# Layer 1's experts on their chosen rows only: routing and scattering inside the first plain cross attention, then 39 blocks of 512 rows from a table made on the chip

## The reference, cut to what matters

```python
x = x + L1_xattn(layernorm(x), ctx, ...)        # 16 heads, 77 keys a sequence
x = x + L1_ffn(layernorm(x), ...)

def L1_ffn(xt):                                  # 8192 tokens; D = H = 128, E = 8, K = 2
    scores = softmax(xt @ gate_w.T)              # over 8 experts
    top_vals, idx = top_k(scores, 2)
    xs = xt[:, None, :] * top_vals[:, :, None]
    for e in range(8):
        mask = (idx == e)
        h  = silu(xs @ w1[e].T + b1[e])
        x2 = h @ w2[e].T + b2[e]
        x3 = xs @ w3[e].T + b3[e]
        y += sum over k of x2 * x3 * mask
    z = (silu(xt @ sw1.T) * (xt @ sw2.T)) @ sw3.T   # shared expert, 256 wide
    return y + z
```

## Time and profile before

| what | value |
|---|---|
| time, median of 3 runs | 4141.17 us (4141.11 to 4141.33) |
| the profiled execution's own time | 4179.66 us |
| its span in the trace | 4177.9 us |
| PE busy over the span | 3262.2 us, 78% |
| DVE busy | 3183.3 us, 76% |
| ACT, POOL busy | 2340.8 us (56%), 1688.6 us (40%) |

### The profile page before, as it was taken

One profiled execution on the slowest core, in us unless ns is written; L12 is line 12 of the kernel. 1 busy time (PEld: TensorE's weight loads), 2 busy tenths in 40 slices (PEclk: granted clock), 3 DMA queues, 4 the chain that ended last, 5 costly groups with the idle time before them and its releaser, 6 DMA issues. The chain is left out here.

```text
span 4177.9 us, 77148 instructions
## 1 busy us (share of the span) xinstructions
PE 3262.2 (78%) x23624; PEld 1971.2 (47%) x23624; DVE 3183.3 (76%) x12412; ACT 2340.8 (56%) x4408; POOL 1688.6 (40%) x1692
## 2 busy tenths in 40 slices
PE   4777776999899969999979996886777777676168
PEld 1222222444477744444456664554555555554056
DVE  6999996666588865556578875886999999997055
ACT  5999995333366634444446654664666666665020
POOL 5777773000100012222244444223246666666650
PEclk9999998999899989999999998998555555655575
DMA  2000004100000000000000000000001100000037
GB/s 71 5 5 5 5 5 174 70 1 1 7 9 8 9 25 1 1 1 1 1 17 15 15 13 4 2 2 11 12 27 46 39 18 6 5 4 2 9 95 203
DMA packets 112625, 98.97 MB, mean 24 GB/s; under 512 B 65004, under 2 KB 95928, under 8 KB 109277
## 3 DMA queue, kind: packets, MB, share of 16 engines
q1 hardware_dynamic: 88670, 78.97, 6.7%
q0 software_dynamic: 14336, 10.87, 0.8%
q10 hardware_dynamic: 9216, 4.20, 0.4%
HBM read 55.57 MB, written 57.97 MB: 27 GB/s over the span
## 5 line engine op out<-in xcount | busy, mean ns | idle before, releaser
L393 PE MATMUL PS<-IDENT,a_T 128*77 128x128 f32 (+1 forms) x3584 | 618.0, 311 | 149.1 <-ACT a_Pr L528 115.4
L1012 ACT ACTIVATE l_H<-l_H 128x2048 f32<-128x2048 f32 (+2 forms) x256 | 597.9, 2719 | 2.8 <-POOL l_H L1064 2.7
L393 PEld LDWEIGHTS PS<-IDENT,a_T 128*77 128x77 f32 (+1 forms) x3584 | 480.4, 170 | 249.1 <-issue 91.7
L1064 POOL TENSOR_TENSOR l_H<-l_feat,l_text 128x4096 f32<-128x4096 f32 x64 | 450.6, 7041 | 131.0 <-PE PS L968 130.3
L968 PE MATMUL PS<-l_H,l_wide 128*32 128x512 f32 (+1 forms) x2560 | 331.9, 594 | 165.4 <-ACT l_H L1012 165.3
L1086 DVE TENSOR_TENSOR l_H<-PS,l_text 128x2048 f32<-128x2048 f32 (+1 forms) x192 | 411.6, 2146 | 2.1 <-ACT l_text L1039 2.1
L530 ACT ACTIVATE a_Pr<-PS 77x512 f32<-77x512 f32 (+1 forms) x640 | 375.3, 587 | 53.9 <-PE PS L393 53.7
L408 PE MATMUL PS<-a_Pr,a_vaug 77*32 77x128 f32 (+1 forms) x7168 | 307.2, 317 | 7.6 <-issue 3.1
L2099 POOL DMA_INDIRECT expert_rows<-e3r_row,e3r_rows_at x256 | 254.3, 993 | 86.6 <-issue 73.5
L616 POOL TENSOR_TENSOR a_T<-a_mx,a_T 128x616 f32<-128x616 f32 x128 | 155.7, 1217 | 313.9 <-DVE a_mx L682 313.8
L338 PE MATMUL PS<-a_kblk,a_qT 32*128 32x308 f32 (+1 forms) x2048 | 238.6, 540 | 23.9 <-ACT a_kblk L542 6.6
(11 more groups left out here) (302 smaller groups left out, 8307.1 us busy)
## 6 DMA issues: line engine op xcount, KB each, us to landing
expert_shares<-e_zero SPq DMA_DIRECT2D x16, 1024.0 KB, 22.6
e3c_four<-expert_shares SPq DMA_DIRECT2D x64, 256.0 KB, 3.3
e_w<-in_L_ffn_w SPq DMA_DIRECT2D x14, 512.0 KB
e3x_xin<-expert_rows SPq DMA_DIRECT2D x32, 200.0 KB
expert_rows<-e_zero SPq DMA_DIRECT2D x6, 1024.0 KB, 8.7
a_cT<-in_ctxT SPq DMA_DIRECT2D x128, 38.5 KB, 1.8
X<-in_x SPq DMA_DIRECT2D x8, 512.0 KB, 7.2
expert_rows<-e3r_row,e3r_rows_at POOLq DMA_INDIRECT x256
```

The lines of the kernel that those rows point to most:

```text
L393: last = pe.transpose(PS[0:keys, 4 + g % 2, j * S:(j + 1) * S], T[:, u, c:c + keys], m.IDENT[:, :])
L1012: act.activation(cells, cells, ACT.Tanh).then_inc(q[f"tanh{part}"], 1)
L1064: pool.tensor_tensor(H[:, a, lo * S:hi * S].rearrange("p (t f) -> p t f", f=S), bcast(feat[:, a, :], 1, hi - lo), bcast(text[:, a, lo:hi], ...
```

## The change

**A router inside layer 1's cross attention.** attention_layer gets hooks. Each group of four sequences is routed in stages at fixed distances behind the attention: stage n of group i runs at step s = 4i + 6 + n, so a stage comes once in four steps, and after the last sequence the hooks run on alone, for steps 67 to 80. The stages: n=0 POOL, deviations of the four sequences (ten small operations); n=1 ACT, four normalised copies; n=2, 3 PE, four transposes; n=3, 4 PE, four logit products of 8 columns, in front of `project_out`; n=5 to 9 DVE, some 25 small operations (softmax over 8, the eight largest of each token, the marks of the two chosen, keys and row numbers); n=7, 9 POOL, a few small operations; n=8 PE, 14 bfloat16 products of 8 columns that count the pairs ahead of each in its expert's region, again in front of `project_out`; n=10, 11 ACT and POOL, four scaled copies each of the rows (weight times token); n=11 to 14 POOL, eight indirect transfers of 128 rows of 528 bytes (128 values, then the number of the pair) to `pair_rows`, a table of 69632 rows in HBM with one region for each expert.

**Blocks.** After the cross attention a product gives the count of each expert, and 13 small DVE operations make a table of 39 blocks: the expert and the first row of each. 39 blocks always run (16384 pairs need 32 full blocks, and at most 7 partly filled ones more). SP loads each block's expert weights (128 by 1552 bytes) and its 512 rows, with addresses read from the table, four buffers deep. PE turns the rows (four transposes), does gate, value and down (three float32 products of 512 columns) and turns the result back (four transposes); ACT copies and does the silu, DVE adds biases and multiplies, and POOL scatters the 512 results with four indirect transfers to `pair_shares`, two rows for each token. The shared expert of the first six groups is cut into 18 pieces, one behind each second block.

**Adding up.** When all results are sent, SP loads 16 times 512 KB of them; DVE adds the two shares of each token to X and takes statistics (`add_places`), among the shared expert's pieces of the ten groups left. The widening, the accumulation on POOL and the products of the experts that were not chosen are gone.

**Zeros.** `clear_rows` fills `pair_rows` (36.8 MB) too, ahead of the two tables of layer 3 (23.6 MB).

The diff, cut to its core:

```diff
@@ -811,17 +825,28 @@
                     return
                 if real(fin):
                     residual(fin, (v - lag - 2) % 2)
+                if router is not None:
+                    router.vector_first(dve, s)
+                if real(fin):
                     statistics(fin)
                 if real(s):
                     subtract_max(s, u, h, 0)
+                if router is not None:
+                    router.vector_second(dve, s)
                 if real(end):
                     norm_heads(end, (v - lag - 1) % 2)
+                if router is not None:
+                    router.vector_third(dve, s)
                 if real(s):
                     subtract_max(s, u, h, 1)
+                if router is not None:
+                    router.vector_fourth(dve, s)
                 if real(s + 1):
                     place_v(s + 1, (v + 1) % slots)
                     if k_ready == "k":
                         spread_k(s + 1, a)
+                if router is not None:
+                    router.vector_last(dve, s)
...
             def project_out(i, u):
@@ -427,6 +433,8 @@
                 if not topk:
                     pe.wait_ge(q[k_ready], q.nth(k_ready, i, -(lag + 2)))
                 pe.wait_ge(q["v"], q.nth("v", i, -(lag + 2)))
+                if router is not None:
+                    router.tensor_projected(pe, i + lag + 2)
                 if inner is None:
                     last = pe.matmul(out_ps, OT[:, u, :], Wo[:, :], start=True, stop=True)
                 else:
...
-def layer1_experts(nc, m, t):
+PAIR = 2
...
-            def widen(i, u, e):
-                if e == 0:
-                    pe.wait_ge(q["partsTs"], q.nth("partsTs", i))
-                if past_part(i, e, E, 1):
-                    pe.wait_ge(q["xs"], nth_part(i, e, E, 1))
-                pe.matmul(PS[:, 2, :], pick[:, e * 128:(e + 1) * 128], r.partsT[:, u, :],
-                          start=True, stop=True).then_inc(q["wide"], 1)
...
+    def tensor_projected(pe, s):
...
+            pe.wait_ge(m.at["x"], m.at.nth("x", min(s - 4, B - 1)))
+        projected_read(pe, s - 1)
+        i = due(s, 8)
+        if i is not None:
+            u = i % 2
+            pe.wait_ge(q["mask"], i + 1)
+            if i >= 1:
+                pe.wait_ge(q["ahead"], i)
+            for g in range(G):
+                out = PS[:, 7, 416 + g * E:416 + (g + 1) * E]
+                pe.matmul(out, before[:, :], mask[:, u, g * E:(g + 1) * E], start=True, stop=False)
+                for c in range(g):
+                    pe.matmul(out, ones[:, :], mask[:, u, c * E:(c + 1) * E], start=False, stop=False)
+                last = pe.matmul(out, ones[:, :], ahead[:, u, :], start=False, stop=True)
+            last.then_inc(q["pos"], 1)
+        for half in range(2):
+            i = due(s, 3 + half)
+            if i is not None:
+                pe.wait_ge(q["yT"], 2 * i + half + 1)
+                for j in range(2):
+                    g = 2 * half + j
+                    last = pe.matmul(PS[:, 7, 384 + g * E:384 + (g + 1) * E],
+                                     yT[:, (G * i + g) * S:(G * i + g + 1) * S], gate[:, :], start=True, stop=True)
+                last.then_inc(q["logits"], 1)
+    r.tensor_projected = tensor_projected
...
+                           -1.5, None, ALU.is_lt).then_inc(q["mask"], 1)
...
+    def scatter(pool, i, g):
+        if i == 0 and g == 0:
+            pool.wait_ge(m.s_cleared, m.cleared)
+        pool.wait_ge(q["at"], i + 1)
+        pool.wait_ge(q["xs0"], G * i + g + 1)
+        pool.wait_ge(q["xs1"], G * i + g + 1)
+        for k in range(K):
+            pool.indirect_dma_start(
+                out=m.pair_rows[:, :],
+                out_offset=bass.IndirectOffsetOnAxis(ap=rows_at[:, i % 2, g * K + k:g * K + k + 1], axis=0),
+                in_=rows_of(i)[:, g, k, :], in_offset=None,
+                bounds_check=PAIR_ROWS - 1, oob_is_err=False).then_inc(q[f"scat{i % 2}"], 16)
+    def pool_first(pool, s):
+        i = due(s, 7)
+        if i is not None:
+            chosen(pool, i)
+    r.pool_first = pool_first
+    def pool_end(pool, s):
+        i = due(s, 0)
+        if i is not None:
+            deviations(pool, i)
+        i = due(s, 9)
+        if i is not None:
+            addresses(pool, i)
+        for half in range(2):
+            i = due(s, 10 + half)
+            if i is not None:
+                second_rows(pool, i, half)
+        for g in range(G):
+            i = due(s, 11 + g)
+            if i is not None:
+                scatter(pool, i, g)
+    r.pool_end = pool_end
...
+        i = due(s, 7)
+        if i is not None:
+            dve.wait_ge(q["best2"], i + 1)
+            if i >= 1:
+                dve.wait_ge(q["mask"], i)
+            dve.sem_inc(q["passed"], 1)
+            for g in range(G):
+                last = dve.match_replace(mark[:, g * (E + PAD):(g + 1) * (E + PAD)], best[:, 8 * g:8 * g + 8],
+                                         ex[:, g * (E + PAD):(g + 1) * (E + PAD)], -2.0)
+            last.then_inc(q["marked"], 1)
+        i = due(s, 8)
...
+                dve.wait_ge(q["marked"], i)
+            dve.sem_inc(q["passed"], 1)
+            for g in range(G):
+                last = dve.max(best[:, 8 * g:8 * g + 8], ex[:, g * (E + PAD):g * (E + PAD) + E])
+            last.then_inc(q["best"], 1)
...
+                dve.wait_ge(q["at"], i)
+            dve.sem_inc(q["passed"], 1)
+            for g in range(G):
+                last = dve.max(keytop[:, 8 * g:8 * g + 8], skey[:, g * E:(g + 1) * E])
...
+        EARLY = 6
+        def piece_after(b):
+            return (b // 2 // 3, b // 2 % 3) if b >= 0 and b % 2 == 0 and b // 2 < 3 * EARLY else None
...
+        def _(sp):
+            sp.wait_ge(q["table"], 2)
+            for b in range(BLOCKS):
+                v = b % V
+                if b >= V:
+                    sp.wait_ge(q["prod"], b - V + 1)
+                e = sp.value_load(table[0:1, b:b + 1], min_val=0, max_val=E - 1)
+                sp.dma_start(w[:, v, :], t[n + "blocks"][bass.ds(e, 1), :, :].rearrange("a p c -> p (a c)")) \
+                    .then_inc(q[f"w{v}"], 16)
+                if b >= V:
+                    sp.wait_ge(q["rT"], b - V + 1)
+                    sp.wait_ge(q["at"], b - V + 1)
+                slot = sp.value_load(table[0:1, BLOCKS + b:BLOCKS + b + 1], min_val=0, max_val=PAIR_ROWS - BLOCK)
...
+            for v in range(V):
+                sp.wait_ge(q[f"sent{v}"], len(range(v, BLOCKS, V)) * (G * 16))
+            for i in range(NG):
+                if i >= 3:
+                    sp.wait_ge(q["sum"], i - 2)
+                sp.dma_start(four[:, i % 3, :].rearrange("p (g c) -> p g c", g=G),
...
+            def lift(b):
+                pe.wait_ge(q["xT"], b + 1)
+                pe.wait_ge(q[f"w{b % V}"], b // V * 16 + 16)
+                if b >= 1:
+                    pe.wait_ge(q["hid"], b)
+                pe.matmul(PS[:, 1, :], w[:, b % V, 0:D], xT[:, b % 2, :], start=True, stop=True).then_inc(q["gate"], 1)
+                if b >= 1:
+                    pe.wait_ge(q["up"], b)
+                pe.matmul(PS[:, 2, :], w[:, b % V, 2 * D:3 * D], xT[:, b % 2, :], start=True, stop=True) \
+                    .then_inc(q["value"], 1)
+            def down(b):
+                pe.wait_ge(q["hid"], b + 1)
+                if b >= 1:
+                    pe.wait_ge(q["prod"], b)
+                pe.matmul(PS[:, 3, :], w[:, b % V, D:2 * D], hid[:, b % 2, :], start=True, stop=True) \
+                    .then_inc(q["down"], 1)
...
+            def turn_back(b):
+                pe.wait_ge(q["prod"], b + 1)
+                if b >= 1:
+                    pe.wait_ge(q["res"], b)
+                else:
+                    pe.wait_ge(q["count"], 1)
+                for g in range(G):
+                    last = pe.transpose(PS[:, 4, g * D:(g + 1) * D], prod[:, b % 2, g * S:(g + 1) * S], m.IDENT[:, :])
+                last.then_inc(q["back"], 1)
...
+                    turn_rows(b + 1)
+                if b >= 0:
+                    down(b)
+                if b + 1 < BLOCKS:
+                    lift(b + 1)
+                if b >= 0:
...
+            def multiply(b):
+                dve.wait_ge(q["down"], b + 1)
+                dve.wait_ge(q["up"], b + 1)
+                if b >= 2:
+                    dve.wait_ge(q["back"], b - 1)
+                dve.scalar_tensor_tensor(out=prod[:, b % 2, :], in0=PS[:, 3, :],
+                                         scalar=w[:, b % V, 3 * D + 1:3 * D + 2], in1=up[:, b % 2, :],
...
+            def add_places(i):
+                f4 = four[:, i % 3, :].rearrange("p (g k d) -> p g k d", k=K, d=D)
+                dve.wait_ge(q[f"four{i % 3}"], i // 3 * 16 + 16)
+                dve.wait_ge(q["x"], i + 1)
+                dve.tensor_tensor(xg(i), xg(i), f4[:, :, 0, :], ALU.add).then_inc(q["added"], 1)
+                dve.wait_ge(q["added"], i + 1)
```

(20 more changed lines are left out.)

756 lines of the change are left out of this document (520 added, 236 removed).

## The result

The changed kernel takes 3985.47 us (median of 4 runs, 3982.48 to 3990.43) beside 4141.25 us before (4 runs, 4141.11 to 4141.62): a ratio of 0.9625, interval 0.9608 to 0.9642, or -155.8 us. The forecast was 4006 us, -135, in a range of 3945 to 4115. One thing has to be known to read what follows: the device of this comparison and that of the last experiment ran the kernel before in 4141 to 4144 us; the three devices of the other experiments took 4178 to 4180 for the same kernel, and the profiled execution of before (a span of 4177.9 us) is like theirs. I call these the 4141 and the 4180 devices, and compare only within one kind; what makes the two kinds is not known.

The account below looks back on a forecast made before the run. PE's chain of float32 products was taken to bound layer 1's experts. Removing that 579.4 us stage and adding terms of 444 us gave -135.4 us, from 4141.2 to 4006 us, range 3945 to 4115.

Parts of the forecast that it names:

- Blocks: 39 expert blocks of layer 1: POOL's four scatters at 1.28 us set each at 5.12 us, 200 us in all.
- Tail: Router after the last residual: 30 transfers left plus copies, deviations and marks on POOL alone, uncovered, 51 us.
- Start: From the router's end into the blocks: wait to first row turned 12.6, table 4.2, first results 6.2; 23 us.
- Prelude: Start of layer 1's cross attention: ten more loads on SP ahead of the first context load, 4.5 us.
- Adding up: After the blocks: 16 additions among ten groups of shared pieces, 7.3 us a period, 85 us; bounds 59 and 121.
- Cross attention: Layer 1's cross attention with the router inside: 4.65 us more per four steps, 16 groups, 75 us; bounds 32 and 120.
- +0.9 of DVE between two halves: Cross attention step where n=4 and n=8 fall: 0.9 us of DVE in line beside 1.2 of PE, counted as +2.4.
- the forecast's lower sum of 2.0: Cross attention, per group: PE's lower sum alone in line, DVE's work in the gaps, 2.0 us; gives the 32 us bound.
- The 0.4 a group for the port: Cross attention: small DVE operations with two SBUF inputs stand while POOL holds SBUF, +0.4 us a group.
- the falling clock: Rival in blocks and adding up: TensorE's clock falls; at 0.79 blocks +12 us, at 0.58 4130 us total; 7%.
- DVE did not lock them: Rival in the blocks: DVE locks POOL out of writing descriptors, 7.9 us a block, +108 us, 4114 us total; 4%.
- the 240 of the rival: Rival in layer 1's cross attention: clock falls to 0.58, +15 us a group, +240 us, 4246 us total, slower; 6%.

Follow-up runs that it names:

- the last experiment: Changed kernel with every scattered row number past the table's end, so the blocks' four scatters write nothing; 3981.2 us, one run (kernel before 4143.6).
- half of the rows: Changed kernel without the router's scatter of each token's second row, 64 of 128 transfers left out; 4054.9 us, one run on a 4180 device.
- The 4099 measured there: The changed kernel itself, unedited, run on a 4180 device against the kernel before; 4099.0 us, ratio 0.9811.

## Why the forecast was right, point by point

- **Blocks, 200 against 199.0.** Right, and for the reason given: four scatters of 1.28 on POOL's queue. The half of them gave PE's 168.2, where the forecast had 168; its terms give 39 x 4.22 = 165.
- **Tail, 51 against 54.1.** Right in mechanism (half of the rows: 33 us). POOL's copies of rows cost 0.61 each and not 0.456, and the transfer behind a copy 1.36 us in place of 1.28.
- **Start, 23 against 24.4.** Right as a sum, but by two errors against each other. From the last scatter's end to the first row turned, with the table, it had 12.6 + 4.2 = 16.8 us and it took 12.8: in layer 3 it was 7.5 us to the next row of any engine (3948.94 to 3956.48), here 3.9 (to 1626.10); from there to the first scatter it had 6.2 and it took 11.6, with PE's clock at 1.2 GHz until 1642.7, behind a tail in which PE was busy 17 of 75 us:

```profile
1635.00 1.12 PE L2081 MATMUL PS<-IDENT,e_xin 128*128 128x128 f32 x4 [8.70 <-DMA e_xin<-pair_rows]
```

- **Prelude, 4.5 against 1.9; landing and first load, 5.5 against 5.3.** Right within 3 us. The cross attention's first load starts 1.25 us earlier than before (1111.39 against 1112.64), so the ten loads cost 3.2 us; the rest of their 4.7 is hidden.
- **Adding up, 85 against 89.1.** The period was to be 7.3; six are 7.56 us, two 8.9 and the first 10.25, and in these three the granted clock is at 1.2 GHz for a part. DVE's wait for the small products, 2.14 us in a period of 7.56, is the chain as described.
- **Cross attention, 75 against 48.9.** This is the mis-sized term, 26 us too much; the other terms take 5 of it back, and 21 are left as the miss. The step that failed is "+0.9 of DVE between two halves" together with "+0.2, +0.65 and +1.0" for the other steps: I let most of DVE's 4.8 us a group stand in line, where DVE costs 0.5. PE's part was right: 1.9 us a group in line (0.73, and 1.19 with the counting) beside the forecast's lower sum of 2.0. Two readings of the rows were behind it. The sum of durations on DVE is near (4.65 us a group), but they make it busy for only 2.0 us more; and the idle time was taken from two gaps, 0.84 us a step, where the earlier trace rows has 67 us in 60 steps, 1.12 a step. The first of the four steps doesn't add up either: 1.2 and 0.9 are 2.1 and not 2.4. In all 2.4 us a group in place of 4.65, near the lower bound of 32 us: 38.8 where the clock held. The 48.9 has some 10 us of drops of the clock in it, for which the sum had no term, and they brought the measured time nearer to the forecast by luck. The 0.4 a group for the port was next to nothing. The Trainium skill ("SBUF — State Buffer", Who interferes with whom) has this contention for two SBUF inputs beside a GpSimd read; the trace has it beside L1731 in before, once beside L618 in after, and beside transfers hardly (one operation of 411 ns in place of 178).
- **Zeros, 0.** Right: the filling ended before 840 us, the forecast had 845, and the cross attention starts no later than before.
- **The rivals.** The clock in the blocks stayed at 1.00, with eight transposes in each, so the falling clock did not come; POOL's scatters never passed 980 ns, so DVE did not lock them; the clock of the cross attention did drop, but for some 3 us at a time and 11 us in all, not the 240 of the rival. The rival of the falling clock had its 0.79 from layer 3's blocks, and that was the 4180 device: on the 4141 device the same blocks run at 0.97.
- **What was not foreseen** is that a 4180 device takes back 75 of the 156 us; nothing in the forecast stood for it. The 4099 measured there would still lie in the range, but for none of the reasons that made it so wide, and that the forecast was set beside a 4141 device is luck. The profiled execution of before held the sign: it was 38.5 us above the median, with 27 "remote" waits in layer 3, and the sum took that difference as if it had no stage of its own. The rows of layer 3 that it used for the blocks' pace (1.28 us a scatter) are the same on both kinds; its clock is not.

## What to carry to other kernels

Cost an insertion into a pipelined loop by the engine that stands last in the chain: here PE's products and transposes ahead of the output product were time almost whole, and of some 4.7 us of small DVE operations 0.5 was. An indirect transfer of 128 rows cost its queue 1.28 us whether it wrote or not; count the queue's transfers first, and fill the engines that wait for them with work from elsewhere, as the shared expert's pieces in the tail and the blocks. When a profiled execution is well above the median, find which stage holds the difference before using its rows; waits for a releaser called "remote" in a program on one core were the sign here.
